# An LSTM step with attention: both sums of exponentials on VectorE, the first alpha's copy on ScalarE

## The reference, cut to what matters

```python
def attend(h):
    q = h @ Wq.T
    scores = jnp.einsum('bc,bsc->bs', q, context)
    alpha = jax.nn.softmax(scores, axis=-1)
    ctx = jnp.einsum('bs,bsc->bc', alpha, context)
    return jnp.tanh(jnp.concatenate([ctx, h], axis=-1) @ Wout.T + b_out)

def step(carry, x_t):
    h, c, attn = carry
    inp = jnp.concatenate([x_t, attn], axis=-1)
    gates = inp @ W_ih.T + b_ih + h @ W_hh.T + b_hh
    i, f, g, o = jnp.split(gates, 4, axis=-1)
    c = jax.nn.sigmoid(f) * c + jax.nn.sigmoid(i) * jnp.tanh(g)
    h = jax.nn.sigmoid(o) * jnp.tanh(c)
    attn_out = attend(h)
    return (h, c, attn_out), attn_out
```

## Time and profile before

| what | us |
|---|---|
| median of 3 runs | 6038.66 |
| lowest and highest run | 6036.6, 6039.16 |
| span of the profiled execution | 6037.1 |
| the loop over the steps, within that span | 262 to 4228 |
| TensorE busy, whole span | 5442.3 |
| VectorE busy, whole span | 3651.2 |
| ScalarE busy, whole span | 2098.9 |

### The profile page before, as it was taken

The page is one execution under the profiler, slowest core; times in us unless marked ns, Lnnn a source line. Parts: engine busy times, 40 slices in busy tenths (PEclk is TensorE's granted clock), DMA queues, the critical chain, the costliest instruction groups (busy, mean ns, idle before and its releaser), DMA issues. The chain is left out here.

```text
span 6037.1 us, 384310 instructions
## 1 busy us (share of the span) xinstructions
PE 5442.3 (90%) x171160; PEld 3792.5 (63%) x171160; DVE 3651.2 (60%) x16434; ACT 2098.9 (35%) x7989; POOL 353.7 (6%) x811
## 2 busy tenths in 40 slices
PE   6899999999999999999999999999788888787989
PEld 2577777777777777777777777777544344334433
DVE  4355555555555555555555555555488999999931
ACT  3144444444444444444444444444222122223221
POOL 0000000000000000000000000000011211112000
PEclk8999999999999999999999999999888889898989
DMA  1100000000000000000000000000221111111111
GB/s 69 58 2 2 2 2 2 2 2 2 2 2 2 2 2 2 2 2 2 2 2 2 2 2 2 2 2 2 84 62 40 45 31 40 38 42 36 47 39 54
DMA packets 45131, 111.57 MB, mean 18 GB/s; under 512 B 8160, under 2 KB 10208, under 8 KB 44528
## 3 DMA queue, kind: packets, MB, share of 16 engines
q1 hardware_dynamic: 43600, 109.39, 5.9%
q10 hardware_dynamic: 1440, 1.06, 0.1%
HBM read 99.90 MB, written 10.52 MB: 18 GB/s over the span
## 5 line engine op out<-in xcount | busy, mean ns | idle before, releaser
L711 PE MATMUL lstm_part_ps<-lstm_keys,lstm_hid 128*4 128x128 f32 x32768 | 1025.2, 273 | 206.2 <-DVE lstm_hid L880 206.2
L727 PE MATMUL lstm_ctx_ps<-lstm_values,lstm_alpha 128*4 128x128 f32 (+1 forms) x49152 | 1052.0, 237 | 0.2 <-issue 0.2
L711 PEld LDWEIGHTS lstm_part_ps<-lstm_keys,lstm_hid 128*4 128x4 f32 x32768 | 770.7, 86 | 429.8 <-DVE lstm_hid L880 415.7
L727 PEld LDWEIGHTS lstm_ctx_ps<-lstm_values,lstm_alpha 128*4 128x4 f32 x49152 | 901.4, 86 | 94.5 <-issue 0.4
L909 DVE TENSOR_REDUCE lstm_neg_max<-lstm_part_ps 128x1 f32<-128x128 f32 x1024 | 298.6, 292 | 679.5 <-PE lstm_part_ps L711 679.5
L842 ACT ACTIVATE lstm_expo<-lstm_part_ps,lstm_neg_max 128x128 f32<-128x128 f32 x1024 | 375.9, 367 | 863.5 <-DVE lstm_neg_max L909 863.5
L670 PE MATMUL lstm_half_ps<-lstm_w_hid,lstm_hid 128*13 128x96 f32 x16384 | 595.8, 246 | 0.0
L862 DVE STREAM_TRANSPOSE lstm_gates<-lstm_half_ps 128x96 f32<-128x96 f32 x1026 | 290.2, 283 | 397.3 <-PE lstm_half_ps L670 373.2
L670 PE MATMUL lstm_half_ps<-lstm_w_attn,lstm_attn 128*13 128x96 f32 x16448 | 525.8, 248 | 0.0
L670 PEld LDWEIGHTS lstm_half_ps<-lstm_w_attn,lstm_attn 128*13 128x13 f32 x16448 | 300.1, 93 | 155.7 <-ACT lstm_attn L855 107.0
L1945 ACT ACTIVATE mix_gated<-mix_gate_ps 115x512 f32<-115x512 f32 (+2 forms) x200 | 112.6, 563 | 778.5 <-PE mix_gate_ps L1673 778.4
(11 more groups left out here) (325 smaller groups left out, 8500.5 us busy)
## 6 DMA issues: line engine op xcount, KB each, us to landing
mix_ring<-in_sm_chunks SPq DMA_DIRECT2D x120, 358.0 KB, 2.9
mix_ring<-in_mix_chunks SPq DMA_DIRECT2D x80, 384.0 KB, 3.0
lstm_xg<-xg_rows SPq DMA_DIRECT2D x514, 16.0 KB
xg_rows<-lstm_xg_tile SPq DMA_DIRECT2D x16, 512.0 KB, 2.6
ctxT<-in_ctxT SPq DMA_DIRECT2D x1, 2048.0 KB, 14.6
out_xT<-xT SPq DMA_DIRECT2D x4, 512.0 KB, 3.8
xT<-in_xT SPq DMA_DIRECT2D x1, 1536.0 KB, 9.7
lstm_w_x<-in_lstm_w_x SPq DMA_DIRECT2D x1, 1024.0 KB, 10.0
```

What stands on the lines that cost most here:

```text
L711: mm = pe.matmul(part_rows(score_ps[part], b), hid[:, k, lo:lo + SPACE], keys[:, k, b * SRC + c * P:b * SRC + (c + 1) * P], start=(n == 0 ...
L727: mm = pe.matmul(part_rows(ctx_ps[n], b), alpha[:, b, c, SPACE - 1 - c:2 * SPACE - 1 - c], values[:, b * SC + c, ctx_cols[n]], start=(c == ...
```

## The change

ScalarE's exponentials no longer give a sum. VectorE makes both sums with a reduction over `expo` in SBUF (`sum_part`), the first behind the minimum of the maxima, the second behind the copy of the second alpha, and the totals' spread now follows the second sum. The copy of the first alpha moves from VectorE to ScalarE, between the two exponentials. The copy of the second stays on VectorE and comes ahead of the totals' spread. The semaphore of the alphas becomes two.

```diff
--- before.py
+++ after.py
@@ -615,7 +615,8 @@
             inverse_ready = q.sem("lstm_inverse_ready")
             factor_ready = q.sem("lstm_factor_ready")
             alpha_turned = q.sem("lstm_alpha_turned")
-            alpha_ready = q.sem("lstm_alpha_ready")
+            alpha_ready = [q.sem(f"lstm_alpha{part}_ready") for part in range(PARTS)]
+            total_part_ready = q.sem("lstm_total_part_ready")
             ctx_ready = [q.sem(f"lstm_ctx{n}_ready") for n in range(PIECES)]
             out_row_ready = [q.sem(f"lstm_out_row{o}_ready") for o in range(KC)]
             attn_summed = [q.sem(f"lstm_attn{o}_summed") for o in range(KC)]
@@ -641,6 +642,12 @@
 
             def by_part(ap):
                 return ap.rearrange("p (a c) -> p a c", a=PARTS)
+
+            def alpha_rows(part):
+                return alpha[:, :, 2 * part:2 * part + 2, SPACE - 1]
+
+            def turned_rows(part):
+                return turned_ps[part].rearrange("p (b r) -> p b r", r=2)
 
             @block.sync
             def _(sp):
@@ -787,14 +794,14 @@
                         turn(0)
                         hidden_part()
                         half_hid(0, 0)
-                        pe.wait_ge(alpha_ready, 2 * t + 1)
+                        pe.wait_ge(alpha_ready[0], t + 1)
                         for n in range(PIECES):
                             context(0, n)
                         pe.wait_ge(exp_ready, 2 * t + 2)
                         turn(1)
                         for n in range(PIECES):
                             context(1, n)
-                        pe.wait_ge(alpha_ready, 2 * t + 2)
+                        pe.wait_ge(alpha_ready[1], t + 1)
                         for n in range(PIECES):
                             context(2, n)
                             context(3, n).then_inc(ctx_ready[n], 1)
@@ -839,8 +846,11 @@
                             act.activation(tanh_c[:, k, :], cell[:, k, GATES - 1, :], ACT.Tanh, scale=0.5).then_inc(c_tanh[k], 1)
                         for part in range(PARTS):
                             act.wait_ge(max_ready, 2 * t + part + 1)
-                            act.activation(expo[:, part, :], score_ps[part], ACT.Exp, bias=neg_max[:, part:part + 1],
-                                           accum_out=total[:, part:part + 1]).then_inc(exp_ready, 1)
+                            act.activation(expo[:, part, :], score_ps[part], ACT.Exp, bias=neg_max[:, part:part + 1])\
+                               .then_inc(exp_ready, 1)
+                            if part == 0:
+                                act.wait_ge(alpha_turned, 2 * t + 1)
+                                act.copy(alpha_rows(0), turned_rows(0)).then_inc(alpha_ready[0], 1)
                         act.wait_ge(max_all_ready, t + 1)
                         act.activation(by_part(shrink[:, :]), spread_values(spread_max[:, :]), ACT.Exp, scale=-1.0,
                                        bias=neg_max_all[:, :]).then_inc(shrink_ready, 1)
@@ -880,10 +890,10 @@
                     dve.scalar_tensor_tensor(out=by_batch(hid[:, k, PAD:]), in0=by_batch(o_col[:, k, :]), scalar=1.0,
                                              in1=tanh_c[:, k, :], op0=ALU.add, op1=ALU.mult).then_inc(h_ready[k], 1)
 
-                def keep_turned(t, part):
-                    dve.wait_ge(alpha_turned, 2 * t + part + 1)
-                    turned = turned_ps[part].rearrange("p (b r) -> p b r", r=2)
-                    dve.tensor_copy(alpha[:, :, 2 * part:2 * part + 2, SPACE - 1], turned).then_inc(alpha_ready, 1)
+                def sum_part(t, part):
+
+                    dve.wait_ge(exp_ready, 2 * t + part + 1)
+                    dve.tensor_reduce(total[:, part:part + 1], expo[:, part, :], AX_X, ALU.add).then_inc(total_part_ready, 1)
 
                 for ps in (*half_ps, *part_ps, *ctx_bank):
                     dve.memset(ps[:, :], 0.0)
@@ -908,15 +918,17 @@
                             dve.wait_ge(scores_ready, 2 * t + part + 1)
                             dve.tensor_reduce(neg_max[:, part:part + 1], score_ps[part], AX_X, ALU.max, negate=True)\
                                .then_inc(max_ready, 1)
-                        keep_turned(t, 0)
                         dve.wait_ge(max_ready, 2 * t + 2)
                         dve.transpose(spread_blocks(spread_max[:, :]), every_row(neg_max[:, :])).then_inc(max_spread, 1)
                         dve.wait_ge(max_spread, t + 1)
                         dve.tensor_reduce(neg_max_all[:, :], spread_values(spread_max[:, :]), AX_XY, ALU.min)\
                            .then_inc(max_all_ready, 1)
-                        dve.wait_ge(exp_ready, 2 * t + 2)
+                        sum_part(t, 0)
+                        dve.wait_ge(alpha_turned, 2 * t + 2)
+                        dve.tensor_copy(alpha_rows(1), turned_rows(1)).then_inc(alpha_ready[1], 1)
+                        sum_part(t, 1)
+                        dve.wait_ge(total_part_ready, 2 * t + 2)
                         dve.transpose(spread_blocks(spread_total[:, :]), every_row(total[:, :])).then_inc(total_spread, 1)
-                        keep_turned(t, 1)
                         dve.wait_ge(shrink_ready, t + 1)
                         dve.wait_ge(total_spread, t + 1)
                         dve.scalar_tensor_tensor(out=by_part(weighed[:, :]), in0=by_part(shrink[:, :]), scalar=1.0,
```

## The result

The changed kernel takes 6294.48 us (median of 4 runs, 6293.48 to 6295.64) against 6038.8 us before (median of four runs, one more than in the table above), a ratio of 1.0427 with a 95% interval of 1.0414 to 1.044: 256 us slower, or 0.50 us in each of the 512 steps. The forecast was 6310 us (6249 to 6358). The profiled execution has a span of 6293.6 us.

A forecast was written before the change was run, and what follows sets the result against it. TensorE's context chain released the scaling, the normaliser having 0.16 us of cover. Second copy 0.04 us earlier, then sum, transpose and waits: scaling from 10.75 to 11.28, 0.53 us times 512, 271 us more, so 6310 us (6249 to 6358).

The forecast's parts named there:

- Where the cost lies: Normaliser chain on VectorE, 0.16 us of cover: second sum, transpose and waits behind the second copy; scaling 0.53 us later a step.
- The second sum: VectorE's reduction of 128 elements behind the second alpha's copy: claimed to take 0.29 us, from 9.87 to 10.16.
- The first copy on ScalarE: First alpha's copy between the exponentials: 0.18 us long, ready 0.04 us sooner, second exponential hardly moved.
- VectorE started it right behind the second maximum: First alpha's copy before the change: started at 8.84, right behind the second maximum that ran from 8.56 to 8.85.
- How much earlier the second copy comes: Second alpha's copy on VectorE: claimed to start 0.04 us earlier, at 9.79, following the second turn.
- The wait in front of `weighed`: On VectorE behind the totals' transpose: `weighed`, with two waits, claimed to start 0.07 us behind it, bounds 0.03 to 0.09.
- At the scaling: ScalarE's scaling of the context, L849, with two waits: claimed to start 0.09 us behind the factor, 0.03 at least.
- The rest of the step is rigid: From the scaling through `select(0)` to tanh and the next gates: the 0.53 us delay counted in full each step.
- A sum held until the copy's end: Rival: VectorE does not overlap the second sum with the copy in front; 46 us more, 6356 us, chance 5%.
- The clock stayed at 1.00: Rival: the clock falls to 0.88 in the recurrence; 384 us more, near 6690 us, chance 3%.
- ScalarE's copy was not slow: Rival: first alpha's copy takes 0.30 us and holds the second exponential; 61 us more, 6371 us, chance 4%.
- The signs: Listed trace marks: scaling waits for the factor, period 8.28 us, sums 0.29 us, VectorE waits less before the copy.

## Why the prediction was right

- *Where the cost lies.* The normaliser's chain, with 0.16 us of cover, got the second sum, the transpose and two waits behind the second copy, and became what the scaling waits for. The releaser changed hands as forecast, the second sum taken away gives back the 0.31 us from its start to the transpose's (6.88 to 7.19), done twice it costs its length less the overlap, and the first sum, done 0.21 us before the second copy starts, costs nothing.
- *The second sum.* Estimated at 0.29, it takes 0.28 us (277 ns mean).
- *The first copy on ScalarE.* It takes 174 ns where 0.18 was taken, and does not hold the second exponential, which starts at 5.95, 0.33 behind the second maximum's start, as before. But the step "VectorE started it right behind the second maximum" gave the wrong reason for 8.84: the turn held it. With the read gone VectorE's own copy is as early as ScalarE's, to 0.01 us.
- *How much earlier the second copy comes.* This term was mis-sized: 0.04 forecast, 0.10 measured. I put 0.10 us between the first turn's end and the copy, from the second turn; the rows show 0.07 there (5.74 to 5.81; before it was 0.06, 8.78 to 8.84), so that the 0.09 us of the accumulator's read came through whole.
- *The wait in front of `weighed`.* Mis-sized the other way: 0.07 taken, 0.03 to 0.09 as bounds, 0.10 measured. At the scaling 0.09 was taken and 0.10 measured.
- *The rest of the step is rigid.* `select(0)` starts 0.42 us behind the scaling, as before (8.31 to 8.73; 10.75 to 11.17), and the step grew by just the 0.50 us by which the scaling moved. The sum of the two misses, 0.06 less and 0.03 more, is the 0.03 us a step, 15 us, by which the forecast was high.
- *The rivals.* A sum held until the copy's end: the rows show it starting 0.09 us behind the copy's start (6.79, 6.88), while the copy ran to 6.96, much as `weighed` had. The rule of the Trainium skill's page "VectorE: DVE Perf Modes", section "The DRAIN you can't avoid", that the next operation waits for an empty pipe, isn't what this trace shows for a copy and a reduction that does not need it. The same section adds that a next operation that is not held (one that need not wait for the earlier ones) starts earlier. The trace agrees with that, and the prediction left it out. The clock stayed at 1.00. ScalarE's copy was not slow.
- *The signs.* Those named as right came, the period with 8.25 us for 8.28 and the sums with 0.28 us for 0.29, but for one: VectorE was to wait less in front of the second copy, and it waits 0.21 us, as before (6.79; 9.83 in the earlier trace rows).

## What to carry to other kernels

Ask of each new instruction not which engine has room but which chain it stands in, and how much later that chain may end: here VectorE was 60% busy, the sum of part 0 was free in a gap of its queue, and the same instruction one place further down cost its length 512 times. Where an operation can be done as soon as its input is there, put it ahead of the wait that follows, and not behind it, as long as it ends before that wait does: the two sums ahead of the copy ended at 9.86, and the copy started at 9.88. Of two waits on one instruction, write the one that ends last first where it is on the critical chain, and check that the chain really is: the same edit was worth 0.07 us at `weighed` and 0.06 at the scaling, and nothing at a third place.

## What was not expected of the hardware

An instruction with two waits starts 0.03 to 0.04 us behind the end of what it needs if the late wait is written first in this program, and 0.10 us behind it if it is written last (`weighed` 7.44 to 7.54 in the changed kernel, 4.48 to 4.51 with the order turned round; the scaling 8.21 to 8.31, and 5.19 to 5.23). On the path of each step that is 61 us of the changed kernel's 256 (194 above before with both turned round).

In the view by source line of the changed kernel (count, ns, first and last start) these are the waits for the totals (L933) and for the factor (L858):

```profile
L933 DVEq EVENT_SEMAPHORE  x512: 21/21/21, 265.1 to 4482.4; - x171
L858 ACTq EVENT_SEMAPHORE  x512: 17/17/17, 265.9 to 4483.2; - x171
```

In the step shown above, L933 of the changed kernel starts at 7.47, 0.04 us behind the transpose's end, and `weighed` starts 0.05 us behind the end of L933: the two stand in a row. With the order turned round L933 is the wait for `shrink`, and it starts at 4.25, while the transpose runs; `weighed` then waits for the transpose alone. So which wait stands apart comes from how the program is built, and the 0.07 us are what a late wait that stands apart costs in these traces. Whether both waits could be put on one instruction isn't shown.
